# Attention's first latents made in the last FFN block, score products ahead of value products, another order of the shared units

## What is computed

```python
# layer 2
gate = silu(x @ Wg.T); up = x @ Wu.T
x = layernorm(x + (gate * up) @ Wd.T)
# layer 3, S = 256, 16 heads, latents of 192 (queries) and 64 (keys and values), 64 rotary features
cq = rms_norm(x @ w_qa.T, q_a_ln_w)
q = (cq @ w_qb.T).reshape(b, s, 16, 192)          # 128 plain, 64 rotary (rope)
ckv = x @ w_kva.T
k_pe = rope(ckv[..., 64:]); ckv_l = rms_norm(ckv[..., :64], kv_a_ln_w)
kv = (ckv_l @ w_kvb.T)                            # keys and values of each head
scores = where(causal, -inf, q @ k.T * 192 ** -0.5)
x = layernorm(x + softmax(scores) @ v @ w_o.T)
# layer 4, of which the change moves the shared part
shared = silu(x @ shared_gate.T) * (x @ shared_up.T) @ shared_down.T
x = layernorm(x + routed_experts(x) + shared)
```

## Time and profile before

| | us |
|---|---|
| median of 3 runs | 1982.46 (1981.31 to 1984.31) |
| profiled execution | 1981.61, of which span 1979.80 |
| TensorE busy | 1842.4 (93% of the span) |
| VectorE, ScalarE, GpSimd busy | 1483.6, 1038.8, 835.4 |
| recurrence, FFN with head products, attention, experts (first matmul) | from 0, 743.3, 966.7, 1799.4 |

### The profile page before, as it was taken

How to read it: one execution, slowest core, us unless ns; L and a number is a source line. 1 busy time by engine, 2 the same in 40 slices (tenths; PEclk the granted TensorE clock), 3 DMA queues, 4 the chain that set the end, 5 groups by cost and what they waited for, 6 DMA issues and landing times. The chain is left out here.

```text
span 1979.8 us, 35608 instructions
## 1 busy us (share of the span) xinstructions
PE 1842.4 (93%) x12032; PEld 1647.6 (83%) x12032; DVE 1483.6 (75%) x4074; ACT 1038.8 (52%) x2694; POOL 835.4 (42%) x865
## 2 busy tenths in 40 slices
PE   7999999999999999999799999999999999978980
PEld 5788888888888888888589999999999999967980
DVE  8978778787878785665477888888888888864436
ACT  5434333333333333333277777777777777734653
POOL 1222323222332220000144466666666666655775
PEclk9999999999999999999799999999999999999995
DMA  3201000010101005573100010000000000126867
GB/s 126 87 1 33 10 24 22 11 32 1 33 1 50 30 22 159 175 248 123 30 12 17 18 41 28 21 21 20 19 19 19 20 19 14 39 74 180 205 136 257
DMA packets 102003, 118.81 MB, mean 60 GB/s; under 512 B 12567, under 2 KB 93723, under 8 KB 101184
## 3 DMA queue, kind: packets, MB, share of 16 engines
q1 hardware_dynamic: 89104, 108.42, 17.1%
q0 software_dynamic: 12288, 8.11, 2.7%
q10 hardware_dynamic: 432, 0.02, 0.0%
HBM read 75.50 MB, written 57.10 MB: 67 GB/s over the span
## 5 line engine op out<-in xcount | busy, mean ns | idle before, releaser
L282 POOL TENSOR_TENSOR kept_q_rows<-kept_q_rows 128x512 f32<-128x512 f32 x128 | 203.6, 1591 | 526.5 <-DVE kept_q_rows L547 526.5
L1569 POOL TENSOR_TENSOR kept_raw<-kept_raw,mla_row_inv 128x512 f32<-128x512 f32 x192 | 199.6, 1039 | 258.5 <-DVE mla_row_inv L1916 257.2
L372 ACT ACTIVATE kept_q_rows<-rwkv_r 128x512 f32<-128x512 f32 x128 | 76.7, 600 | 399.0 <-DVE rwkv_o_low L468 396.3
L1728 ACT ACTIVATE kept_raw<-kept_raw,mla_least 128x256 f32<-128x256 f32 (+1 forms) x512 | 227.7, 446 | 74.7 <-DVE mla_least L1900 73.4
L1900 DVE CUSTOM_DVE_ANT_0 kept_raw<-mla_score,kept_mask 128x256 f32<-128x256 f32 (+1 forms) x512 | 156.8, 352 | 83.3 <-PE mla_score L2275 52.8
L532 DVE TENSOR_TENSOR kept_q_rows<-rwkv_v,kept_q_rows 128x512 f32<-128x512 f32 x128 | 88.0, 688 | 111.7 <-PE rwkv_v L583 108.6
L539 DVE TENSOR_TENSOR_SCAN rwkv_state<-rwkv_decay_w,kept_q_rows 128x256 f32<-128x256 f32 x256 | 166.5, 692 | 4.1
L1654 POOL DMA_INDIRECT slots<-mla_x_out,mla_slot_now x128 | 130.0, 1016 | 30.8 <-issue 24.2
L1744 ACT ACTIVATE mla_p_high<-mla_turn 128x512 fp32r<-128x512 f32 x192 | 114.0, 594 | 46.0 <-PE mla_turn L2283 44.6
L1910 DVE TENSOR_TENSOR mla_p_low<-mla_turn,mla_p_high 128x512 fp32r<-128x512 f32 x192 | 128.0, 667 | 0.6 <-ACT mla_p_high L1744 0.6
L2283 PE MATMUL mla_turn<-kept_ident,kept_raw 128*128 128x128 f32 x768 | 115.8, 273 | 8.8 <-DVE mla_p_low L1910 8.8
(11 more groups left out here) (487 smaller groups left out, 6283.7 us busy)
## 6 DMA issues: line engine op xcount, KB each, us to landing
kept_raw<-in_experts SPq DMA_DIRECT2D x27, 384.0 KB
kept_raw<-in_rkvo SPq DMA_DIRECT2D x16, 512.0 KB
moe_y_in<-sums SPq DMA_DIRECT2D x32, 256.0 KB, 4.8
sums<-ffn_empty SPq DMA_DIRECT2D x12, 512.0 KB
slots<-ffn_empty SPq DMA_DIRECT2D x16, 361.2 KB
moe_e_rows<-slots SPq DMA_DIRECT2D x31, 180.6 KB
kept_x_in<-x SPq DMA_DIRECT2D x18, 256.0 KB, 18.2
mla_x_res<-x SPq DMA_DIRECT2D x17, 256.0 KB
```

The source lines that it names most:

```text
L282: nc.gpsimd.tensor_tensor(gate[:, c % 2, :], key[:, c % 2, :], gate[:, c % 2, :], ALU.mult).then_inc(gated_done, 1)
L1569: nc.gpsimd.tensor_tensor(unit, unit, row_inv[:, v % PR, 0:len(heads)].rearrange("p (h a) -> p h a", a=1) .to_broadcast([P, len(heads), ke ...
L1728: last = nc.scalar.activation(probs[:, v % PR, i * keys:(i + 1) * keys], masked[:, v % 2, i * keys:(i + 1) * keys], ACT.Exp, bias=least[:, ...
```

## The change

Three things are done.

1. The latents of sequence 0 are made inside the FFN's last block. `ffn_phase` gets tiles and semaphores for it and writes to `cq_part`, `k_part`, `k_first` and `k_rows`, which now are kept tiles; the two banks of `xt_ps` take the products. TensorE turns the rows after step 0 (`turn_first`), makes the latents after step 1 (`latents`), and turns them after step 4 (`turn_latents`). ScalarE splits and squares at steps 0 and 2, and copies the turned latents behind the last `h_high`; GpSimd takes the root ahead of the last block's power; VectorE splits at step 0, scales at step 3, and subtracts behind the last `h_low`. SyncE loads the second sequence's rows as soon as the first's are turned. Attention's head begins with `transpose_x(1)` and the queries.
2. The head products: for each group of four heads all score products, then all value products, with a semaphore step for each kind. Copies and subtractions of the scores wait for the scores alone. `multiplied_low(0)` stands ahead of the last `apply_norm`.
3. Shared units: in the odd half TensorE makes the up product first, then turns the next unit, then makes the output product of the unit before; the even half holds the gate product alone. VectorE makes `unit_hidden` ahead of the next unit's `unit_low`, and `add_shared` of the unit before follows in the odd half. ScalarE's order is as it was.

```diff
@@ ffn_phase: sync
             over_blocks(sp, body)
+            sp.wait_ge(first_turned, 1)
+            sp.dma_start(x_first[:, :, :], x2[SEQ:2 * SEQ, :].rearrange("(t p) d -> p t d", p=P)).then_inc(second_in, 16)
             store(NB - 1)
@@ ffn_phase: gpsimd
             def body(blk, first, last):
+                if last:
+                    latent_rstd()
                 pool.wait_ge(var_done, blk + 1)
...
@@ ffn_phase: scalar
+                    if last and j == 0:
+                        first_turn_high()
+                    if last and j == 2:
+                        latent_squares(0)
+                        latent_squares(1)
             over_block_pairs(act, body)
             h_high(HC * NB - 1, HC - 1)
+            latent_turns_high()
             for g in range(HEADS // HG):
                 multiplied_high(g)
             def multiplied_high(g):
-                act.wait_ge(multiplied, g + 1)
+                act.wait_ge(multiplied, 2 * g + 1)
                 nc.scalar.activation(wq_high[:, :, g * HG * KVL:(g + 1) * HG * KVL],
...
+                act.wait_ge(multiplied, 2 * g + 2)
                 nc.scalar.activation(wvo_part[0][:, 2 * g:2 * g + 2, :],
@@ ffn_phase: vector
+                    if last and j == 0:
+                        first_turn_low()
+                    if last and j == 3:
+                        latent(0)
+                        latent(1)
             h_low(HC * NB - 1, HC - 1)
+            latent_turns_low()
             layer_norm(NB - 1)
+            multiplied_low(0)
             apply_norm(NB - 1)
-            for g in range(HEADS // HG):
+            for g in range(1, HEADS // HG):
                 multiplied_low(g)
@@ ffn_phase: tensor
+                    if last and j == 0:
+                        turn_first()
+                    if last and j == 1:
+                        latents()
+                    if last and j == 4:
+                        turn_latents()
+            def latents():
+                pe.wait_ge(first_high, 1)
+                pe.wait_ge(first_low, 1)
...
+            def turn_latents():
+                pe.wait_ge(lat_done, 2)
...
                     for k in range(2):
-                        nc.tensor.matmul(score[:, k * SEQ + i * KVL:k * SEQ + (i + 1) * KVL],
...
+                        last = nc.tensor.matmul(score[:, k * SEQ + i * KVL:k * SEQ + (i + 1) * KVL],
...
+                last.then_inc(multiplied, 1)
+                for i in range(HG):
+                    raw = raw_heads[g][:, i, :]
                     at = (i % 2) * KVL
@@ attention_phase: sync
-            sp.wait_ge(turn_filled, X0 + 1)
-            sp.dma_start(x_rows[:, :, :], seq_rows(x2, 1)).then_inc(rows_in, 16)
@@ attention_phase: gpsimd
-            latent_rstd(0)
-            latent_rstd(1)
@@ attention_phase: vector
-            split_turn("x", 0, 0)
-            latent(0, 0, LAT_PS[0])
-            latent(1, 1, LAT_PS[1])
-            split_turn("cq", 0, 0)
-            split_turn("k", 0, 0)
+            split_turn("x", 0, 1)
             values_low(0, 0)
-            split_turn("x", 0, 1)
...
-                if half is not None and half % 2 == 0 and half >= 2:
-                    add_shared(half // 2 - 1)
+                if half == 2 * EARLY:
+                    add_shared(EARLY - 1)
                 elif half is not None and half % 2 == 1:
+                    unit_hidden(half // 2)
                     if half // 2 + 1 < EARLY:
                         unit_low(half // 2 + 1)
-                    unit_hidden(half // 2)
+                    if half >= 3:
+                        add_shared(half // 2 - 1)
                     unit_hidden_low(half // 2)
@@ attention_phase: tensor
-            transpose_x(0)
-            wait_turned(pe, "x", 0, 0)
-            latents(0, 0, LAT_PS[0])
-            latents(1, 1, LAT_PS[1])
-            transpose_cq(0)
-            transpose_k(0)
             transpose_x(1)
-            wait_turned(pe, "cq", 0, 0)
             for c in range(4):
                 queries(0, c, QUERY_PS[c])
...
-                    if half >= 2:
-                        unit_out(half // 2 - 1)
+                    else:
+                        unit_out(EARLY - 1)
                 elif half is not None:
+                    unit_in_matmul(half // 2, 1, score_ps[1], up_ready, hidden_done)
                     if half // 2 + 1 < EARLY:
                         turn_unit(half // 2 + 1)
-                    unit_in_matmul(half // 2, 1, score_ps[1], up_ready, hidden_done)
+                    if half >= 3:
+                        unit_out(half // 2 - 1)
```

193 lines of the change are left out of this document (151 added, 42 removed).

## The result

The changed kernel takes 1964.13 us in the median (1962.01 to 1970.99, 4 runs), the kernel before in the same session 1983.19 (1981.31 to 1984.31). The ratio is 0.9908, with an interval of 0.9895 to 0.9922: 19 us by the medians, 18 by the ratio (15.5 to 20.8). The forecast was 15.1 us less and 1967.4; its range holds the time. The profiled execution is the longest of the four: 1970.99, with a span of 1969.1.

What follows compares the result with a forecast made beforehand. Attention's head was taken as bound by latency at a lowered clock, FFN's block by TensorE, attention's end by a routing chain. 16.2 - 2.9 - 1.7 + 3.5 = 15.1 us less gave 1967.4, range 1963.5 to 1973.5.

Steps and rivals of the forecast that it cites:

- Part 1: Attention's head without the first latents: last head product to second sequence's latents 7.47 us at full clock, gain 16.2.
- Part 2: FFN's last block: added latent matmuls and transposes cost TensorE 2.9 us, the rest hidden; bound 5.72.
- Part 3: Other order of the head products ahead of attention: worth 0, bounds 1.2 us either way.
- The clock: Attention's head: one fall, 3.4 us at 1.2 GHz, does 1.7 us less work, taking 13.3 to 11.6.
- The rival: Clock stays up through the 2.35 us gap ahead of attention: 16.8 us gained, 1965.7; chance 0.25.
- Part 4: End of attention, new order of shared units: routing finishes earlier, gain 3.5 us, cap 4.2, floor -3.
- places at 1777.8 and the last scatter 3.5 us earlier: End of attention: routing matmuls called places, at 1781.36 before, start at 1777.8; GpSimd's last scatter comes 3.5 us earlier.
- experts start less than 2 us earlier against that steady part: Sign of being wrong: experts' start, measured against the end of attention's steady part, gains under 2 us.
- Sum: Whole kernel: 11.6 + 3.5 = 15.1 us less, 1967.4 forecast.

Runs made afterwards that it cites:

- matched profiles: Second profiles of the changed kernel (span 1965.8) and of the kernel before (span 1983.0), both unchanged; ratio 0.9907 for the changed kernel.
- before_again: The kernel before as it stands, profiled a second time; span 1983.0 us.
- narrow_scores: The kernel before, each score product taking only 64 of its 128 stationary columns, so all are 64 wide; 0.45 us a head.
- wide_values: The kernel before, head products in old order, value products' stationary matrices 128 columns wide instead of 64; 0.88 us a head.
- successor: The changed kernel with longer runs of one kind in the head products and two low parts ahead of the last norm's statistics; 0.9884, median 1961.18 us.
- first pair: First profiles of the kernel before and the changed kernel; spans differ by 10.7 us, the medians (1983.19 and 1964.13) by 19.
- one_bank: As wide_values, with the value products written into the scores' PSUM bank, over them; 0.88 us a head.
- two_heads: The kernel before, head products two heads at a time: four score products, then two value products; 0.81 us a head, 3.2 a group.
- filled: The successor plus matmuls nobody reads, 8 behind the last head product and 36 behind the last shared unit; 0.9904.

## Why the prediction was right, and where it wasn't

- **Part 1** held in each of its terms. Gap 2.48 for 2.35; transposition and queries as at full clock, plus one stretch of 3.4 us at 1.2 GHz: 9.15 for 9.17 (7.47 + 1.7). Its reason for the gap was right too: copies take 1.37 for 1.35, and the barrier 1.11 behind VectorE for 1.00.
- **Part 2** held: 2.84 for 2.9, and no wait at any of the three pieces. The FFN as a whole is 3.3 longer between the matched profiles; the 0.4 left is within what its steps vary by (203.19 us in before_again, 203.77 in narrow_scores, with the same code and the same falls).
- **Part 3** is the step that failed: "a piece of scores and a piece of values each take 0.58 from start to start ..., 32 of these in a row, so the sum doesn't depend on the order: 0", with bounds of 1.2. It was worth 6.3 us, wait of 0.57 included. The bound counted 12 changes; there were 31 and 7 are left, so 24 fall away. But even 24 at 0.1 would be 2.4 us. The 0.58 was not the price of a piece, it was the price of a piece behind one of the other kind, because the rows had no other: it held the change of width (0.29 us a head by wide_values), and it kept two neighbouring value products from running as a pair. Two score products of 64 columns and one value product of 256 at the very same time was the sign, and the loader's 0.39 us of idle time stood in the trace for the asking. The wait ahead of the third group wasn't forecast either: I had named only the store as what stands behind the copy, not TensorE, which wants the bank.
- **The clock**: one fall, as chosen, in three of the four profiles of the change and its successor that can be read for it. The rival, given 0.25, came in one; four executions don't test that chance. Nor does the gap alone decide.
- **Part 4** was mis-sized: 2.4 to 2.7 for 3.5. The step "places at 1777.8 and the last scatter 3.5 us earlier" is right for TensorE; the reckoning let VectorE take the places up as before, and it takes them up 0.5 us later; the scatters take another 0.2.
- By its own sign, "experts start less than 2 us earlier against that steady part", the forecast is wrong on the first pair (61.36 to 59.66, 1.7) and right on the matched one (2.7). The first profile of before had been spared a fall at 1738 that all others but one_bank's had. The sign was set finer than one execution can show.
- **Sum.** 15.1 forecast, 17.2 between matched profiles, 18 to 19 timed. The missing 6.3 were partly made up for by 0.8 of part 4, 0.7 in attention's head and some 2 to 3 ahead of the FFN, in it, in the steady part and the experts, of which no piece is beyond the spread. So the range held partly by luck: with part 3 and part 4 as measured the forecast would have been 5 to 6 us lower, around 1962, below the range's own lower end of 1963.5.

## What to carry to other kernels

A start-to-start time from a strictly alternating sequence is the price of the alternation. Before an order is priced at zero, look for the same instruction in a run of its own kind, and at the weight loader's rows beside it. Group matmuls by the width of their stationary matrix; where they are 64 wide, put behind one another those that write to different halves of the partitions, and check who then waits for the bank. When a gap at a barrier moves, ask which engine came last, SyncE and its stores among them, before the gap is put down to the engine that was changed. And where a verdict hangs on a microsecond or two in one place, take a second profile of the kernel before as well.

## Unexpected of the hardware

- A load of 128 stationary columns behind one of 64 stood 0.38 to 0.39 us, in the kernel before and in two_heads alike; with all loads 128 wide this goes, and a head's products take 0.88 us instead of 1.17.
- Matmuls of 64 stationary columns that write to different halves of the partitions ran side by side: two value products took 0.59 us in two_heads, as long as one in the kernel before, and in narrow_scores a head took 0.45.
- The clock's falls read here lasted 3.4 us or a whole multiple (20.5 us in attention's head of the kernel before), and their places vary between executions of one program: behind the same gap of 2.35 us ahead of the FFN it fell in ten of 14 profiles, behind 2.48 us ahead of attention in three of four.
- Behind a barrier of all engines, TensorE's first matmul came 1.00 to 1.11 us after VectorE's last instruction where VectorE was last (14 profiles ahead of the FFN, 13 ahead of attention), and 1.35 after the landing of a store where SyncE was last (filled).
